# Gate, norm and layer-norm placement in a fused decoder kernel, with one transposed tile of pairs 28 to 41 copied by VectorE

## What is computed

```python
x = x + attn(layernorm(x))                       # causal, 16 heads of 32, q/k/v/o weights and biases
x = x + cross(layernorm(x), ctx, ctx)            # causal, 16 heads, keys = values = ctx, no weights
h = layernorm(x)
shared = relu(h @ W_up.T) @ W_down.T
rw = softmax(top2(h @ W_gate.T))                 # 8 gates
x = x + shared + sum(rw) * (h @ W_expert)
```

## Time and profile before

| | |
|---|---|
| median of three runs | 722.11 us |
| the profiled execution, its own time | 721.66 us |
| its span, first to last instruction | 719.6 us |
| PE busy | 677.8 us, 94% |
| PE weight loads busy | 523.9 us, 73% |
| ScalarE busy | 501.0 us, 70% |
| VectorE busy | 498.8 us, 69% |
| GpSimd busy | 257.8 us, 36% |
| mean granted TensorE clock | 0.990 |

### The profile page before, as it was taken

One profiled execution on the slowest core, in us unless ns is written; L12 is line 12 of the kernel. 1 busy time (PEld: TensorE's weight loads), 2 busy tenths in 40 slices (PEclk: granted clock), 3 DMA queues, 4 the chain that ended last, 5 costly groups with the idle time before them and its releaser, 6 DMA issues.

```text
span 719.6 us, 13877 instructions
## 1 busy us (share of the span) xinstructions
PE 677.8 (94%) x4488; PEld 523.9 (73%) x4488; DVE 498.8 (69%) x1730; ACT 501.0 (70%) x1450; POOL 257.8 (36%) x391
## 2 busy tenths in 40 slices
PE   7998999999999999999969987999989999899998
PEld 6776777767877677677756765777768777577786
DVE  6568666756766676767788789867887669564632
ACT  5678877767876677788899887676688657774110
POOL 3745545333555345751654424433211012000100
PEclk9999999999999999999999998999999999999999
DMA  9663433345433464355956685543363444510101
GB/s 316 171 156 77 125 82 89 75 115 146 117 77 89 117 178 117 84 123 132 273 123 166 158 232 120 148 109 96 88 174 91 113 99 104 141 45 1 58 1 58
DMA packets 52326, 86.12 MB, mean 120 GB/s; under 512 B 8608, under 2 KB 16800, under 8 KB 52256
## 3 DMA queue, kind: packets, MB, share of 16 engines
q1 hardware_dynamic: 52256, 85.25, 45.4%
HBM read 27.55 MB, written 7.34 MB: 48 GB/s over the span
## 4 chain that ended last, share of the span: by engine, by line
PE 77%; DVE 11%; ACT 6%; issue 2%; DMA 2%; POOL 1%; SPq 0%; ACTq 0%; POOLq 0%; DVEq 0%
PE t L480 15%; PE m L519 14%; PE m L520 13%; PE m L521 13%; PE pv L513 10%; PE s L466 8%; DVE probs L680 4%; ACT probs L908 3%; DVE prob L690 1%; DVE xT_lo L766 1%; ACT prob L917 1%; PE m L480 1%; DMA stack<-stage 1%; POOL probs L1021 1%; PE m L583 1%
## 5 line engine op out<-in xcount | busy, mean ns | idle before, releaser
L680 DVE CUSTOM_DVE_ANT_0 probs<-s,mask 128x128 f32<-128x128 f32 (+3 forms) x512 | 245.8, 482 | 135.2 <-PE s L466 132.9
L908 ACT ACTIVATE probs<-probs,negmax 128x128 f32<-128x128 f32 (+3 forms) x512 | 284.7, 559 | 44.6 <-DVE negmax L680 43.3
L480 PE MATMUL t<-ident,probs 128*128 128x128 f32 x1143 | 203.6, 276 | 12.1 <-ACT prob L917 5.0
L917 ACT ACTIVATE prob<-t 128x512 f32<-128x512 f32 (+1 forms) x232 | 125.3, 541 | 109.0 <-PE t L480 108.8
L466 PE MATMUL s<-stack 96*128 96x128 f32 (+3 forms) x512 | 197.5, 392 | 3.8 <-DMA stack<-stage 2.2
L1021 POOL TENSOR_SCALAR probs<-probs,rsum 128x128 f32<-128x128 f32 (+3 forms) x256 | 133.4, 539 | 181.8 <-DVE rsum L694 181.8
L480 PEld LDWEIGHTS t<-ident,probs 128*128 128x128 f32 x1143 | 144.6, 141 | 62.2 <-issue 7.8
L466 PEld LDWEIGHTS s<-stack 96*128 96x128 f32 x512 | 97.4, 190 | 16.5 <-DMA stack<-stage 3.0
L908 ACT ACTIVATION_READ_ACCUMULATOR probs<-probs,negmax 128x1 f32 x512 | 99.1, 194 | 0.0
L690 DVE COPY prob<-t 128x128 f32<-128x128 f32 (+1 forms) x217 | 76.7, 353 | 30.7 <-PE t L480 29.8
L519 PE MATMUL m<-xT_hi,w_lo 128*128 128x512 f32 x192 | 78.4, 409 | 0.9 <-DVE xT_lo L748 0.9
(11 more groups left out here) (144 smaller groups left out, 955.0 us busy)
## 6 DMA issues: line engine op xcount, KB each, us to landing
stack<-stage SPq DMA_DIRECT2D x384, 128.0 KB, 2.3
xt<-in_x SPq DMA_DIRECT2D x16, 256.0 KB, 4.7
xres<-in_x SPq DMA_DIRECT2D x4, 1024.0 KB, 5.9
kraw<-in_ctxT SPq DMA_DIRECT2D x16, 256.0 KB, 3.1
cv<-in_ctx SPq DMA_DIRECT2D x16, 256.0 KB, 3.2
x<-xres SPq DMA_DIRECT2D x3, 1024.0 KB, 5.4
res<-x SPq DMA_DIRECT2D x8, 256.0 KB, 6.3
out<-res SPq DMA_DIRECT2D x2, 1024.0 KB, 4.8
```

The source lines that it names most:

```text
L480: mm = nc.tensor.transpose(dst[:, chunk(qb - kb)], probs[:, (2 * P + h) % 3, OFF[qb] + PART * kb:OFF[qb] + PART * kb + PART], ident[:, :])
L680: nc.vector.tensor_tensor_reduce(probs[:, (2 * P + h) % 3, OFF[qb]:OFF[qb + 1]], score_tile(P, i), mask[:, T - N:T], -SCALE, BIG, ALU.add, ...
L908: nc.scalar.activation(tile, tile, ACT.Exp, bias=negmax[:, P % 2, h, qb:qb + 1], scale=-1.0, accum_out=total).then_inc(p_exp, 1)
L917: nc.scalar.activation(prob[kb][:, 2 * (P % 2) + h, :], turned_tile(P, i), ACT.Copy).then_inc(t_act, 1)
```

## The change

- `FEED`: the FFN of batches 0 and 1 starts four slots later (slots 344 and 408, before 340 and 404). Batches 2 and 3 start where they did (472, 536).
- `FL` jobs at feed +1, +2, +4, +5 in place of +1, +3, +5, +7.
- `FG`: the eight matmuls run first over the four `xT_hi` chunks and then over the four `xT_lo` chunks, each with its own wait, in place of lo and hi of one chunk together after a wait for lo.
- Statistics of norm 6 move from slots 344, 345, 348, 349 to 339 to 342, two of norm 5 from slots 272 and 273 to slot 256 (the other two now both in 272).
- The fourth `L` job of batches 1 to 3 and the fourth `O` job of batches 0 and 1 are one slot later (for batches 2 and 3 of `L`: slot 97 and 161 in place of 96 and 160).
- `turn` of a cross pair waits before each transpose of tile 0 or 4 for the one exponential that it reads, in place of for all four before the first.
- In pairs 28 to 41 (`LIGHT`) tile 1 is copied by VectorE.
- GpSimd gets a wait for norms 5, 6, 7 and for all FFN norms, in the step of each, ahead of its `keys`.

```diff
-FEED = tuple(PAIRS * (PAIRS * (f + B + 1) + 2) + 4 + 4 * (f // 2) for f in range(B))
+FEED = tuple(PAIRS * (PAIRS * (f + B + 1) + 2) + PAIRS for f in range(B))
+LIGHT = range(2 * CROSS_AT[0], PAIRS * (B + 1) + 2)
+def act_turns(P):
+    return (0, 4, 5) if P in LIGHT else T_ACT
+def dve_turns(P):
+    return tuple(i for i in range(PAIRS) if i not in act_turns(P))
+ACT_TURNS = [sum(len(act_turns(p)) for p in range(P)) for P in range(NP)]
...
-        return [z + 24, z + 25, z + 28, z + 29]
-    return [z + 16, z + 16, z + 17, z + 17] if j == B + 1 else [z, z, z + 1, z + 1]
+        return [z + 19, z + 20, z + 21, z + 22]
+    return [z, z, z + 16, z + 16] if j == B + 1 else [z, z, z + 1, z + 1]
...
-                    put(("L", b, t), PAIRS * b - 5, 4 + t + t // 3, 1)
+                    put(("L", b, t), PAIRS * b - 5, 4 + t + 2 * (t // 3), 1)
...
-                put(("O", b, t), PAIRS * (b + 1) + 1 + t, 4 if t < 2 else 0, 4)
+                put(("O", b, t), PAIRS * (b + 1) + 1 + t, (4, 4, 0, 1)[t], 4)
...
-                put(("FL", f, m), 0, u + 1 + 2 * m, 1, 1)
+                put(("FL", f, m), 0, u + 1 + m + m // 2, 1, 1)
...
-                if kb == 0 and not own(P // 2):
-                    pe.wait_ge(p_exp, PAIRS * P + NT * (h + 1))
...
+                    elif kb == 0:
+                        pe.wait_ge(p_exp, PAIRS * P + NT * h + qb + 1)
...
-                    pe.wait_ge(fl_lo, KC * n + c + 1)
-                    nc.tensor.matmul(dst, g_both[:, c, :], xT_lo[:, c, :], start=(c == 0), stop=False)
-                    mm = nc.tensor.matmul(dst, g_both[:, c, :], xT_hi[:, c, :], start=False, stop=(c == KC - 1))
+                    done, x_part = (fl_hi, xT_hi) if c < KC // 2 else (fl_lo, xT_lo)
+                    for k in (2 * c % KC, 2 * c % KC + 1):
+                        pe.wait_ge(done, KC * n + k + 1)
+                        mm = nc.tensor.matmul(dst, g_both[:, k, :], x_part[:, k, :], start=(c == 0 and k == 0),
+                                              stop=(c == KC - 1 and k == KC - 1))
...
-                    if 0 <= s < NP and i in T_DVE:
+                    if 0 <= s < NP and i in dve_turns(s):
...
-                if P % 2 == 0 and h == 0:
+                if P % 2 == 0 and (h == 0 or i - NT not in act_turns(P)):
...
+                for j in range(B + 1, 2 * B):
+                    if s == norm_slots(j)[-1] // PAIRS:
+                        pool.wait_ge(ln_done, NT * (j + 1))
+                for f in range(B):
+                    if s == f_norm_slots(f)[-1] // PAIRS:
+                        pool.wait_ge(f_ln, NT * (f + 1))
```

More of the change, by code:

```diff
@@ L334, in copied @@
         def copied(P, i):
-            if i in T_ACT:
-                return t_act, len(T_ACT) * P + T_ACT.index(i) + 1
-            return t_dve, len(T_DVE) * P + T_DVE.index(i) + 1
+            if i in act_turns(P):
+                return t_act, ACT_TURNS[P] + act_turns(P).index(i) + 1
+            return t_dve, PAIRS * P - ACT_TURNS[P] + dve_turns(P).index(i) + 1
         def emptied(key):
@@ L1001, in _ @@
                         exped(s + 1, i)
-                    if 0 <= s < NP and i in T_ACT:
+                    if 0 <= s < NP and i in act_turns(s):
                         turned(s, i)
```

## The result

| | before | changed |
|---|---|---|
| median | 722.98 us (4 runs, 721.55 to 724.09) | 714.87 us (4 runs, 712.99 to 716.15) |
| ratio to before | | 0.9887, 95% interval 0.9856 to 0.9918 |
| profiled execution | 721.66 us | 715.23 us |
| its span, mean granted clock | 719.6 us, 0.990 | 713.3 us, 0.995 |

Faster, by more than the 0.5% that can be told here. The same two kernels ran once more side by side (experiment 12): 714.57 us (6 runs) against 719.78 (11), 5.2 us less, ratio 0.9916 [0.9898, 0.9933]. The two intervals overlap between 0.9898 and 0.9918, so both readings hold, and 8.1 us is the higher one.

What follows compares the result with a forecast made beforehand. PE, busy for 677.8 us, was taken as the bound, with about 42 us idle to win. Terms -3.2 - 0.8 - 0.2 - 5.3 - 0.4 = -9.9 us took 721.66 to 712 us, range 706.5 to 718.

Steps and rivals of the forecast that it cites:

- L and O: Self-attention, batches 1 to 3: one slot later, the value product covers PE's waits for banks; -3.2 us, bounds 0 and -3.2.
- The 14 copies: Pairs 28 to 41: -0.7 in 353 to 368, +0.5 in 416 to 431, -0.15 in four other windows; sum -0.8 us.
- Exponentials: Cross-pair transposes of tiles 0 and 4: only three transposes ahead of the last save waiting; -0.2 us, bounds 0 and -1.
- Statistics of norm 5: Two move to where VectorE sits idle for 1.67 us and fit; 0, or 1.5 us with cover gone.
- Norm waits: FFN norms of batch 0: with GpSimd held, VectorE wins 2.0 us; the splits behind the wait stay hidden.
- FFN: FFN of batches 0 to 2: moved slots, norm relief and clock give -5.3 us in total; bounds +3 and -10.
- gate order: Last gate: hi first starts about 0.6 us earlier, then runs at ScalarE's pace; -0.4 us, bounds 0 and -1.2.
- Rival C: Only plainly covered waits go, norms and one gate give 2 us, moved FFN slots win nothing: 716.5 us; chance 0.15.
- A: Whole kernel: the main forecast with all its terms, 712 us, own range 708 to 716; chance 0.55.
- The clock: Gated windows at 448.82 and 619.37: the slow 1.2 GHz stretches behind the gates go, 1.4 us each.
- Rival D: PE's clock falls in the longer light stretch and behind it, four more stretches of 1.4 us: 717.7 us; chance 0.06.
- F: The 14 copy pairs: VectorE, ScalarE and PE wait in a loop, about 1 us a pair, 726.8 us; chance 0.04.

Runs made afterwards that it cites:

- experiment 12: The changed kernel once more without an edit, against the kernel before: 714.57 us (6 runs) against 719.78 (11), ratio 0.9916.
- experiments 3: The changed kernel with tile 1 copied by ScalarE in all pairs: 714.44 us against 720.06 for the kernel before, ratio 0.9918.
- 10: The changed kernel with the old FFN slots and no copies moved to VectorE: 714.06 us against 719.78 for the kernel before, ratio 0.992.
- experiment 8: The changed kernel with the FFN of batches 0 and 1 four slots earlier again: 714.85 us against 721.38 for the kernel before, ratio 0.9916.
- experiment 1: The kernel before with only the fourth L job and the fourth O job one slot later: 716.42 us against 720.06, ratio 0.9934.
- 6: The kernel before with only the gate's eight matmuls in the order hi, then lo: 720.89 us against 721.38, ratio 1.0006.
- 7: The kernel before with only the FFN of batches 0 and 1 four slots later: 721.81 us against 721.38, ratio 1.0012.
- experiments 1 and 5: 5 is the kernel before with only GpSimd's waits for the norms: 718.33 us against 721.38, ratio 0.9966.
- experiment 11: The changed kernel with tiles 0 and 4 of pairs 40 to 43 transposed twice: 713.73 us against 719.78 for the kernel before, ratio 0.9906.
- experiment 9: The changed kernel with the old FFN slots and VectorE copies only in pairs 32, 33, 36, 37: 713.34 us against 719.78 for before, ratio 0.9895.
- experiment 2: The kernel before with only the 14 copies of pairs 28 to 41 on VectorE: 722.11 us against 720.06, ratio 1.0018.

## Why the prediction was right in total, and where its terms were not

**L and O: mechanism right, too small.** The -3.2 was also the bound of what can be won, because the waits named in the trace sum to it. PE has no waits left ahead of the value products of steps 12 and 20, as foreseen, and 0.28 us ahead of that of step 4. Measured: -4.7 in the profile, -4.8 alone. The rule "idle time is all there is to win" missed 0.5 us a batch in PE's busy time. How that arises (the ends of pipelined matmuls are modelled) was not tested.

**The 14 copies: the step that failed.** VectorE's price was right, 0.55 us a copy and 0.47 to the next start. Its 14 copies sit where VectorE is idle, ScalarE gains where it is fullest (step 32: -0.75, predicted -0.7). What failed is "in four other windows of these pairs I take -0.15 each", and the 0 for step 34. Both look at the fullness of VectorE, ScalarE and GpSimd; as the traces read, the cost comes from order. A copy ahead of `rsum` delays the start of GpSimd's scaling, an engine busy for 8 of 17 us but at the end of the chain. Measured from step 30 on: +0.9, -0.75, +0.8, -0.3, 0, +0.6: between +0.6 and +1.2 where -0.8 was forecast. The forecast for step 40 was +0.5, for VectorE's norms. The +0.6 there agrees by luck if at all: it comes with a wait for keys grown to 1.79 us, beside DMA at 0.93 of its time, and the window varies as much without the copies. Waits for keys sum to 2.2, 2.6 and 2.7 us in three profiles without the copies (before, experiments 3 and 10), and to 3.4, 2.3 and 2.7 in three with them (changed, experiments 12 and 2).

**Exponentials.** 2.7 us of waits became 0.3, and the windows won nothing. The longest of them stood in step 32:

```profile
361.30 0.66 PE L480 MATMUL t<-ident,probs 128*128 128x128 f32 x4 [1.62 <-ACT probs L908]
```

Experiments 3 and 10 have the single waits and no copies, and their step 32 takes 14.97 us, as before. The forecast -0.2 is 0 in this window; no run has the edit alone.

**Statistics of norm 5.** Forecast 0, and no wait on them appears. Step 34, which two of them left, takes 14.78 and 14.79 us in experiments 3 and 10 against 14.99 before: perhaps -0.2, not tested alone.

**Norm waits: right, and the larger part of the FFN gain.** The norms of 2.01 us fell to 1.00, PE shows no new wait on GpSimd's splits, and the edit alone gives -2.3.

**FFN: over-sized, -5.3 against -2.1.** The failed step is "with three engines at 16 to 17 I expect idle 1.5, not 3.03", and the same 1.5 for slots 464 to 480: with less idle than 3 us each window should have absorbed the moved slots. Idle fell to 2.58 us in both (18.22 less 15.64). The length of slots 400 to 416 came out as foreseen, 18.22 us, by two errors that cancel: forecast 16.7 of work and 1.5 idle, measured 15.64 and 2.58. Slots 464 to 480 were forecast at 17.7 and 1.5, 19.2 in all, and have the same 15.64 and 2.58; that reads as a success until experiment 8, 17.27 us without the shift. There PE is busy for 14.06 us, so the four moved slots of down product cost 1.58 us and not 2.6, and the window absorbed 0.63 of that. The other 0.95 lengthens it, and 0.75 more shows in the neighbour, 21.42 in place of 20.67. So the -2.0 of batch 2 came out as +0.6 at equal clock, the -1.5 of batch 1 as -0.5.

From step 44 to 62 everything can be compared at clock 1.00, and there the changed kernel is 1.2 us shorter than experiment 1. The parts, each from its own experiment: norm waits -0.8, FL slots -0.9 (forecast as a drawback), gate order 0 (the bank waits, not the operand), shift of `FEED` +0.7. They sum to -1.0. In step 42 the norm waits alone gave -1.5 at full clock, and the changed kernel's 23.50 us at 0.86 show none of it against before's 23.40 at 0.85. What the slow clock hides there is open.

**Rival C** (only covered waits and norms count, moved slots win nothing) is nearer to what happened in the FFN than A, and its 716.5 lies within 2 us of the medians 714.87 and 714.57; L and O, larger than either had them, made up the difference. A's 712 is 2.9 us off the first, inside its range.

**The clock.** The forecast had two slow stretches vanish, 1.4 us each. The one at 619.37 did: step 60 runs at 1.00 and takes 20.73 us, 1.36 less. It is slow in four of the six profiles of before and its variants (before, 2, 6, 7) and in none of the eight of the changed kernel and its variants, so this term was probably right. The one in step 42 stayed (0.86). The prediction read one stretch there, behind the gate; the trace of before has two, from about 432 us, ahead of the gate, and from about 449 behind it, and the changed kernel two as well, from 426 and 441. That term failed. Both belong in part to the execution: experiments 1 and 5, with the old gates, had steps 42 and 60 at 1.00. Rival D's mechanism (light use) is what experiment 11 supports, but more stretches than before did not come: leaving out the tail, before had four in its profile and the changed kernel two.

**F, the slower case.** VectorE does wait for PE ahead of a 384-column copy (0.60 us at 336.20), and windows 30 and 34 do grow, but through the reciprocal, by 0.8 to 0.9 us in two windows and not by 1 us in 14 pairs.

**Untried:** the reciprocal ahead of the copy; experiment 9 with the extra PE work of 11; the loads of expert weights and residuals moved out of steps 40 to 42, where DMA is full; the shift for batch 0 alone.

## What to carry to other kernels

Before a small job is given to the engine with spare time, look at what stands behind it in that engine's order: here a 0.5 us copy on an engine two thirds busy delayed the start of a third engine's chain, as far as the traces show, and cost more than it freed. A wait that ends on an operand may still be a wait for the buffer that the operand's reader holds, so changing the order of operands was worth nothing here; follow the job before in the same bank. Work moved by some slots is judged over all windows that it leaves or enters, and at equal clock: experiment 8 looks like a loss of 1.4 us until step 44 and the wait in step 42 are counted.

## What the hardware showed unexpectedly

- PE's clock goes along with most of the spread between runs of one kernel: runs of before had spans of 716.6 us at a mean clock of 0.997 and 719.8 at 0.991, and experiment 2 had 717.8 at 0.997 and 722.4 at 0.985. In the 25 runs of before beside experiments 5 to 8 a straight line through clock and span takes up 78% of the variance. The profiles show between one and five slow stretches each, leaving out the tail, and most of them lie in steps 40 to 44. Two profiles compared without their clocks can differ by 3 us for nothing.
- More work on PE in a light stretch left the kernel no slower, and that window 1.9 us shorter (experiment 11, one profile).
- A pair of 512-column norms on VectorE takes 2.01 us while GpSimd works and 1.00 us while it waits, and holding GpSimd back is a net gain, 2.3 us in the windows and 0.6 to 4.3 by the runs, although GpSimd's own work comes later.
